# One kernel of Mamba scan, experts and linear attention: the two writes of a chunk's bounded last states become one vector instruction

## The reference, cut to what matters

```python
def step(h, inp):                       # h: [batch, 512 channels, 16 states]
    xt, dt, bt, ct, t = inp
    dA = jnp.exp(jnp.clip(dt[..., None] * A, -10.0, 0.0))
    dBx = dt[..., None] * bt[:, None, :] * xt[..., None]
    h = dA * h + dBx
    hn = jnp.clip(jnp.linalg.norm(h, axis=-1, keepdims=True), 1e-06, None)
    scale = jnp.where(hn > 10.0, 10.0 / hn, jnp.ones_like(hn))
    h = jnp.where(t % 16 == 15, h * scale, h)
    y = jnp.einsum('bn,ben->be', ct, h) + D_param * xt
    return (h, y)
```

## Time and profile before

| | us |
|---|---|
| median of 3 runs | 4514.08 (4511.81 to 4515.91) |
| profiled execution, its time | 4514.84 |
| profiled execution, its span | 4512.8 |
| busy in the span: PE, DVE, ACT, POOL | 4253.3, 3632.4, 3057.9, 2588.5 |

### The profile page before, as it was taken

The page is one execution under the profiler, slowest core; times in us unless marked ns, Lnnn a source line. Parts: engine busy times, 40 slices in busy tenths (PEclk is TensorE's granted clock), DMA queues, the critical chain, the costliest instruction groups (busy, mean ns, idle before and its releaser), DMA issues.

```text
span 4512.8 us, 79944 instructions
## 1 busy us (share of the span) xinstructions
PE 4253.3 (94%) x22592; PEld 2960.7 (66%) x22592; DVE 3632.4 (80%) x9610; ACT 3057.9 (68%) x8912; POOL 2588.5 (57%) x1284
## 2 busy tenths in 40 slices
PE   5899999999999999999999999988999999999999
PEld 4777777777777777777777777644444444444444
DVE  3899999999999999999999999855656657566666
ACT  5898888888888888888888888834333332333321
POOL 3988888888888888888888888930000000000000
PEclk8999999999999999999999999999999999999999
DMA  2111111111111111111111111100000000000000
GB/s 101 58 51 62 49 58 53 57 54 57 54 57 54 57 54 57 54 57 54 56 53 54 54 56 55 55 30 22 6 16 16 6 16 6 16 16 7 6 7 10
DMA packets 91560, 187.49 MB, mean 42 GB/s; under 512 B 16160, under 2 KB 58016, under 8 KB 90912
## 3 DMA queue, kind: packets, MB, share of 16 engines
q1 hardware_dynamic: 90272, 180.78, 12.2%
q10 hardware_dynamic: 1152, 5.14, 0.3%
HBM read 168.05 MB, written 17.83 MB: 41 GB/s over the span
## 4 chain that ended last, share of the span: by engine, by line
PE 49%; issue 19%; DVE 18%; POOL 11%; ACT 2%; DVEq 1%; POOLq 0%; DMA 0%; SPq 0%; ACTq 0%
PE ps L684 24%; POOL prod L331 6%; DVE macc L1004 6%; PE ps L658 4%; PE ps L808 3%; POOL hb L339 3%; PE ps L736 2%; PE ps L730 2%; PE ps L750 2%; PE ps L773 2%; PE ps L790 2%; POOL xcv L355 1%; DVE dtt L1189 1%; PE ps_dA L808 1%; PE ps L758 1%
## 5 line engine op out<-in xcount | busy, mean ns | idle before, releaser
L684 PE MATMUL ps<-w_x,mxT 128*128 128x512 f32 x4096 | 1933.7, 601 | 69.6 <-DVE macc L1004 69.6
L1004 DVE SCALAR_TENSOR_TENSOR macc<-ps,gate,macc 128x256 f32<-128x256 f32 x2048 | 977.6, 477 | 498.0 <-PE ps L684 410.0
L915 DVE TENSOR_TENSOR_SCAN hb<-ps_dA,hb 128x1088 f32<-128x1088 f32 x512 | 1240.7, 2423 | 107.4 <-POOL hb L339 99.1
L331 POOL TENSOR_TENSOR prod<-hb,cbc 128x1024 f32<-128x1024 f32 x512 | 1123.1, 2194 | 248.9 <-DVE hb L934 243.5
L339 POOL TENSOR_TENSOR hb<-u,bbc 128x1024 f32<-128x1024 f32 x512 | 1202.0, 2348 | 75.1 <-POOL prod L331 70.9
L394 ACT ACTIVATE zr<-dt,aneg 128x128 f32<-128x128 f32 x4096 | 1240.8, 388 | 1.3 <-DVE dt L1078 1.0
L684 PEld LDWEIGHTS ps<-w_x,mxT 128*128 128x128 f32 x4096 | 727.5, 191 | 739.3 <-issue 604.0
L658 PEld LDWEIGHTS ps<-prod,ident 128*128 128x128 f32 x8192 | 947.5, 192 | 151.9 <-POOL prod L331 91.4
L658 PE MATMUL ps<-prod,ident 128*128 128x128 f32 x8192 | 965.4, 276 | 41.0 <-POOL prod L331 41.0
L403 ACT ACTIVATE ps_dA<-zr 128x1024 f32<-128x1024 f32 x512 | 518.3, 1012 | 0.0
L410 ACT ACTIVATE sq<-hb 128x64 f32<-128x64 f32 x512 | 157.9, 308 | 219.9 <-DVE hb L915 217.4
(11 more groups left out here) (193 smaller groups left out, 4848.3 us busy)
## 6 DMA issues: line engine op xcount, KB each, us to landing
bbc<-bcd SPq DMA_DIRECT2D x128, 512.0 KB, 3.8
cbc<-bcd SPq DMA_DIRECT2D x128, 512.0 KB, 3.7
xt<-in_x SPq DMA_DIRECT2D x128, 128.0 KB, 3.6
x2d<-macc SPq DMA_DIRECT2D x64, 128.0 KB, 1.7
out_dram<-macc SPq DMA_DIRECT2D x64, 128.0 KB, 1.7
w_x<-in_w_x ACTq DMA_DIRECT2D x1, 4096.0 KB, 12.6
hb<-x2d SPq DMA_DIRECT2D x32, 128.0 KB, 2.4
sz<-x2d SPq DMA_DIRECT2D x16, 128.0 KB, 2.2
```

The lines of the kernel that those rows point to most:

```text
L331: TT(dst, states, cc, ALU.mult).then_inc(M["prodp"], 1)
L684: last = mm(banks[p % len(banks)][:], mxT[k][:, j, :], w_x[:, j, p * 512:(p + 1) * 512], start=(j == 0), stop=(j == KD - 1))
L915: V.tensor_tensor_scan(states, dA, states, 0.0, ALU.mult, ALU.add).then_inc(M["scan"], 1)
L1004: STT(macc[k][:], banks[(e // 2) % len(banks)][:, (e % 2) * D:(e % 2 + 1) * D], gate[k][:, e:e + 1], macc[k][:], ALU.mult, ALU.add).then_i ...
```

## The change

The two state buffers become slices of one tensor `hbt`, so that one access pattern reaches column 0 of one and the last column of the other (`ends`, one pattern for each parity of the chunk). `bound` is one SCALAR_TENSOR_TENSOR with an output of 2 x 64 elements a partition: first the next chunk's column 0, then the own last column, both min(factor, 1) times the last states. It reads `nf` and the last states twice. For that `nf` has one factor for each of the 64 rows: ACT's Exp (L420) reads its 4 inputs broadcast and writes 64 elements. `st0` is gone; the scan waits for `hs` in its place. The bound of a tile's last chunk with `carry` keeps two instructions.

```diff
         zr = [sb(f"zr{k}", [P, ST, P]) for k in range(2)]
-        hb = [sb(f"hb{k}", [P, ST, SL]) for k in range(2)]
+        HS = ST * SL
+        hbt = sb("hbt", [P, 2 * HS + 2 * CH])
+        hb = [hbt[:, k * HS:(k + 1) * HS].rearrange("p (a s) -> p a s", s=SL) for k in range(2)]
+
+        ends = (hbt[:, CH:CH + 2 * (HS - CH)].rearrange("p (k r) -> p k r", k=2)[:, ::-1, 0:(ST - 1) * SL + 1:SL],
+                hbt[:].rearrange("p (k r) -> p k r", k=2)[:, :, 0:(ST - 1) * SL + 1:SL])
...
-        nf = trio[:, ST * SL + 16:ST * SL + 16 + EB]
+        nf = trio[:, ST * SL + 16:ST * SL + 16 + ST]
...
                 a.wait_ge(M["nl"], AHEAD + q + 1)
-                a.wait_ge(M["st0"], AHEAD + q)
                 a.wait_ge(M["hs"], AHEAD + q)
-                act(nf, nrl[:], ACT.Exp, scale=-0.5, bias=math.log(10.0)).then_inc(M["ne"], 1)
+                act(nf.rearrange("p (e n) -> p e n", e=EB), nrl[:].rearrange("p (e n) -> p e n", n=1)
+                    .broadcast_to([P, EB, N]), ACT.Exp, scale=-0.5, bias=math.log(10.0)).then_inc(M["ne"], 1)
...
                 v.wait_ge(M["bt"], AHEAD + q + 1)
-                v.wait_ge(M["st0"], AHEAD + q)
+                v.wait_ge(M["hs"], AHEAD + q)
...
                 v.wait_ge(M["ne"], AHEAD + q + 1)
+                if isinstance(top, float):
+                    STT(ends[c % 2], nf.rearrange("p (k m) -> p k m", k=1).broadcast_to([P, 2, ST]), top,
+                        cur[:, :, CH:SL].rearrange("p m k -> p k m").broadcast_to([P, 2, ST]), ALU.min, ALU.mult)                        .then_inc(M["hs"], 1)
+                    return
                 last = cur[:, :, CH:SL].rearrange("p (e n) s -> p e (n s)", e=EB)
-                factor = nf.rearrange("p (e t) -> p e t", t=1).broadcast_to([P, EB, N])
-                STT(nxt[:, :, 0:1].rearrange("p (e n) s -> p e (n s)", e=EB), factor, top, last, ALU.min, ALU.mult)\
-                    .then_inc(M["st0"], 1)
+                factor = nf.rearrange("p (e n) -> p e n", e=EB)
+                STT(nxt[:, :, 0:1].rearrange("p (e n) s -> p e (n s)", e=EB), factor, top, last, ALU.min, ALU.mult)
                 STT(last, factor, 1.0, last, ALU.min, ALU.mult).then_inc(M["hs"], 1)
```

More of the change, by code:

```diff
@@ L134, in rows_of @@
             per = bufs[0].shape[1] * bufs[0].shape[2] // D
-            return bufs[t // per][:].rearrange("p a b -> p (a b)")[:, (t % per) * D:(t % per + 1) * D]
+            return bufs[t // per][:, :, :].rearrange("p a b -> p (a b)")[:, (t % per) * D:(t % per + 1) * D]
         def x_rows(n):
@@ L158, in build @@
         dve_m = ("st1", "mv1", "vp", "den", "sx1", "nx", "keep", "xib", "zb", "xcc", "bcv", "dtb", "dt", "scan", "nr",
-                 "st0", "hs", "yg", "o1", "o2", "st3", "mv3", "vc3", "se3", "r3", "o3", "o4")
+                 "hs", "yg", "o1", "o2", "st3", "mv3", "vc3", "se3", "r3", "o3", "o4")
         act_m = ("xn", "carry", "lnp", "r1", "qs", "xnTs", "ez", "lz", "ss", "ex", "lx", "sx", "edt", "ldt", "zr", "dA", "sq", "nl",
@@ L239, in chunk_product @@
             return (prod[(c // QC) % 2][:].rearrange("p n e t -> p e n t")[:, :, :, tq:tq + CH],
-                    hb[c % 2][:].rearrange("p (e n) s -> p e n s", e=EB)[:, :, :, 1:SL],
+                    hb[c % 2].rearrange("p (e n) s -> p e n s", e=EB)[:, :, :, 1:SL],
                     cbc[c // HC][:, :, t0:t0 + CH].rearrange("p (e n) s -> p e n s", e=1).broadcast_to([P, EB, N, CH]))
@@ L338, in inputs @@
                 t0, half = c * CH, c // HC
-                TT(hb[c % 2][:].rearrange("p (e n) s -> p e n s", e=EB)[:, :, :, 1:SL],
+                TT(hb[c % 2].rearrange("p (e n) s -> p e n s", e=EB)[:, :, :, 1:SL],
                    u[k][:, :, t0:t0 + CH].rearrange("p e (n s) -> p e n s", n=1).broadcast_to([P, EB, N, CH]),
@@ L912, in scan @@
                 v.wait_ge(M["bt"], AHEAD + q + 1)
-                v.wait_ge(M["st0"], AHEAD + q)
-                states = cur[:].rearrange("p a b -> p (a b)")
+                v.wait_ge(M["hs"], AHEAD + q)
+                states = cur.rearrange("p a b -> p (a b)")
                 V.tensor_tensor_scan(states, dA, states, 0.0, ALU.mult,
```

## The result

The changed kernel is slower. The median is 4666.42 us (4661.94 to 4670.78 over 4 runs), against 4514.05 us (4511.81 to 4515.91 over 4 runs) on the same chip: a ratio of 1.0338, with an interval of 1.032 to 1.0356. The forecast was 4499 us and its range ended at 4511 us. The profiled execution took 4670.78 us at a span of 4668.7 us.

The account below looks back on a forecast made before the run. It took a loop of waits between POOL and DVE to bound the scan stage, PE close behind. 0.25 us a tile over 60 tiles gave 15 us, from 4514.84 to 4499.8 and, for the median, 4499 us; range 4488 to 4511 us.

Parts of the forecast that it names:

- The fused form: On DVE, one bound instruction replacing two: 0.335 us in place of 0.43, so `hs` comes 0.10 us earlier.
- the rival of the strided elements: Strided elements cost more: the bound's form takes 0.378 us, saving 0.055 us in 2.5 places, 4506 us; chance 0.11.
- 2.5 places: Places a tile where the saving counts: after bounds 0 and 3, and after bound 7 in every second tile.
- the three places of the sum: After bounds 0, 3 and, in every second tile, 7: a 0.10 us saving there gives 0.25 us a tile.
- the loop of two engines: The tile's path alternating between POOL and DVE: bound 0, POOL, scan 3, bound 3, POOL, scan 7 and `selp`, bound 0.
- the third place: After bound 7, in every second tile, where `dt` hangs on POOL's inputs 1: 0.10 / 2 us a tile.
- the long case of `dt`: `dt` on DVE, between scan 0 and bound 0, lasts 0.66 us in every second tile; predicted near 0.56 us.
- The scan's wait: The scan waits for the whole fused form, starting 0.40 us after the bound began, against 0.39 or 0.34; nothing charged.
- ACT's Exp: ACT's Exp writing 64 elements in place of 4 takes 0.05 us more, covered by DVE's idle time; cost nothing.
- PE: PE close behind with about 1.5 us of room a tile; rival that it sets the pace: 4511 us, chance 0.12.
- A fixed cost: Rival: the fused bound form takes 0.264 us, saving 0.17 us in 2.5 places, 4488 us; chance 0.08.
- two whole ones: Rival: the fused bound form costs 0.53 us, so `hs` is 0.10 us later, 14 us slower, 4528 us; chance 0.07.

Follow-up runs that it names:

- e1_pad32: The changed kernel with 32 semaphore increments that nobody waits for at the head of DVE's queue; 4504.38 us, a ratio of 0.998 to the kernel before.
- e2_before_pad160: The kernel before the change with 160 semaphore increments at the head of DVE's queue; 4643.24 us, a ratio of 1.0285.
- e5_before_pad96: The kernel before the change with 96 semaphore increments at the head of DVE's queue; 4656.75 us, a ratio of 1.0317.
- e9_before_pad128: The kernel before the change with 128 semaphore increments at the head of DVE's queue; 4515.93 us, a ratio of 1.0002.
- e7_forms: The changed kernel with 32 increments, plus 72 extra bound forms at the end of DVE's queue, strided and contiguous; forms timed singly, no kernel time given.
- e6_hybrid: The changed kernel with the fused form only after chunks 0, 3 and 7, two forms elsewhere, and 12 increments; 4512.53 us, a ratio of 0.9994.
- e4_two_forms: The changed kernel with each bound in two forms again, the scan still waiting for `hs`; 4518.38 us, a ratio of 1.0009.

## Why the prediction was wrong

**The step that failed** is "one fewer instruction on DVE free time that isn't on the loop. The buffers' addresses move, nothing else." The instructions' own addresses move too. After and `e1_pad32` differ by 32 increments ahead of the loop alone, and by 4666.4 - 4504.4 = 162 us; `e2_before_pad160` and `e5_before_pad96` bring the same stall into the kernel before. 162 us over 27 branches are 6.0 us each, and the iterations differ by 96.58 - 90.60 = 5.98 us. Of this the gap is 3.77 - 0.30 = 3.47 us. The other 2.5 us come with what follows from it: PE's waits of 1.6 and 2.1 us, the halved clock and the convolution that is then late. In `e1_pad32` PE waits 1.0 us at most, at a mean granted clock of 1.00. In `e2_before_pad160` it is the clock: where it stays at 1.00, the stall costs 3.46 us and PE's waits of 2.0 and 1.1 us nothing. In the changed kernel the clock falls in every steady iteration, so how its 2.5 us divide can't be read there. No rival had the mechanism. What could have led to it was a loop of 373 instructions of which only 80 packets were ever loaded: such a body is held, and whether it stays so after an edit is a question that I didn't put.

The Trainium skill (Runtime: NRT & Kernel Launch, "Instruction fetch mechanics") says that a taken branch whose target lies outside the blocks held waits for a load from memory. The runs agree: 3.5 us a branch. It gives blocks of 256 instructions, two of them held; by that rule `e5_before_pad96` should have been free as `e9_before_pad128` is. It cost 141 us, and its packets have 8192 bytes and start 128 instructions apart, so the measurement decides for four of 128.

**The fused form: right in kind, mis-sized.** I took 0.335 us, for a saving of 0.10 us; the form takes 0.376 us, so 0.43 - 0.376 = 0.054 us. The upper end of 0.378 was the right one, the rival of the strided elements. By my own 2.5 places that is 0.135 us a tile, 8 us over 60 tiles; a tile became 45.473 - 45.294 = 0.18 us shorter by the means of 600 to 2600 us, which is 10.8 us. That the time fell by as much, 10.3, is luck: the scan stage ended 7.0 us earlier (POOL's last instruction at 2980.8 us for 2987.8), and the second stage gave the rest. The guess behind 0.378 had its parts right too. In `e7_forms` 64 more elements at a distance cost 379 - 266 = 113 ns, which leaves 153 ns fixed, where I had 150. What misled was a slope from contiguous rows (291 - 224 = 67 ns for 64 elements) put on a base of strided ones. The Trainium skill's rule of 16-byte lines (Advanced Engine Details and Errata, "SBUF Cachelines") named such a penalty, and `e7_forms` shows one, of about 90 ns on 128 elements.

**Where the 0.05 us counts: partly wrong.** `e6_hybrid` had it at just the three places of the sum and got no gain that can be told from none by its time; its iteration of two tiles is 0.16 us shorter, where the sum with the measured 0.054 us gives 2 x 0.135 = 0.27. The idle times of the scan moved as foreseen (72.0 us in 146 cases became 37.7 in 97, scan 6's is gone), but POOL's waits together fell only from 240.3 to 234.5 us, 0.12 us a tile in place of the 0.2 that I wrote (182.7 + 53.3 + 4.3 before, 154.3 + 53.3 + 26.9 after; a part of the wait for the bound is now put down to PE). The path is not only the loop of two engines that I drew, and what DVE saves in the other chunks counts as well: 0.36 - 0.16 = 0.20 us an iteration, if the longer body of `e6_hybrid` is free, which isn't shown. The sign that I had named for the third place, the long case of `dt` near 0.56 us, proves nothing: its median fell from 0.65 to 0.52 us in `e1_pad32`, but it is 0.52 in `e4_two_forms` too, which gained nothing.

**The scan's wait: mis-sized, but without price.** I had 0.07 us from the end of a form to the scan, hence 0.40 us from the bound's start to the scan's. In `e1_pad32` it is 0.51 us behind most chunks and 0.41 behind chunk 7, here chunks 4 and 7 of one tile:

```profile
1548.59 0.37 DVE L939 SCALAR_TENSOR_TENSOR hbt<-ps_dA,hbt 128x128 f32<-128x128 f32 x1
1549.10 2.42 DVE L923 TENSOR_TENSOR_SCAN hbt<-ps_dA,hbt 128x1088 f32<-128x1088 f32 x1
...
1565.52 0.38 DVE L939 SCALAR_TENSOR_TENSOR hbt<-ps_dA,hbt 128x128 f32<-128x128 f32 x1
1565.93 2.42 DVE L923 TENSOR_TENSOR_SCAN hbt<-ps_dA,hbt 128x1088 f32<-128x1088 f32 x1
```

The difference lies in which instruction carries the wait for `hs`. Behind chunk 7 the scan itself does, and it starts 0.03 us after the form's end, in all 22 cases between 600 and 2600 us. Elsewhere a semaphore instruction of its own carries it, it starts 0.04 us after the form's end, and the scan comes 0.13 us after that end. The earlier trace rows had the 0.13 already: 1529.10 is 0.13 us after the end of the first form at 1528.97. I took the 0.07 us of the other place for both. `e4_two_forms`, with the same wait and two forms, starts its scans 0.565 us after the bound; it was 4 us slower by the medians and 9 us at most by its interval, within what can be told from nothing.

**ACT's Exp: right.** Predicted 0.05 us more and no cost; measured 0.050 us more and a ratio of 1.0002.

**PE: right as far as it went.** In `e1_pad32` PE still follows (its reader waits 9.0 us in 49 cases), and the gain is there. In the changed kernel PE became late by starving, which I had not thought of.

**The rivals.** A fixed cost (0.264) and two whole ones (0.53) fell by the form's 0.376 us. The side was wrong: I gave slower 7 in 100, for a mechanism that isn't there.

## What to carry to other kernels

A change that adds or drops instructions on an engine with a loop moves the body in that engine's instruction store; compare the page's line of the instruction queue before anything else, and look for a wait for "issue" behind the back branch. By these runs a body stays on DVE if it touches no more than three blocks of 128, so one of 373 has 384 - 373 + 1 = 12 good starts in 128 and one of 358 has 27, and a few increments ahead of the loop find them: here 32 of them turned a loss of 3.4% into a gain of 0.2%. A gain of this size needs more than one placement: with 160 increments the loop was as fast, and the whole time could not be told from before. Write strided copies only where the distance is needed, since it cost 0.09 us on 0.29 here.

## What the runs showed of the hardware

- DVE loads its instructions in packets of 8192 bytes, 128 instructions. Three blocks touched by a loop's body: no packet in an iteration. Four: five packets, and 3.5 us more from the branch to the first instruction.
- One stall of 3.5 us cost 6.0 us: PE worked 0.40 of 2 us, and its clock was then granted at 0.50, where the steady part before has a mean of 1.00. In the four iterations of `e2_before_pad160` at a mean of 1.00 it cost 3.46 us.
- 128 elements at a distance of 17 words: 379 ns against 291; 64 elements: 266 against 224.
- On DVE, from an instruction's end to the scan that waits for its signal: 0.03 us where the scan itself carries the wait, 0.13 where a semaphore instruction between them does (`e1_pad32`).
- 128 more increments ahead of the loop take DVE 12.25 us, about 0.1 us each; 8.46 us of that were a wait before, and the start is 4.2 us later.
